# Fused attention and feed-forward block: a slot's projection in two halves instead of four quarters

## The reference

```python
# x: [8, 512, 512]; 16 heads of 32
qkv = einsum('bsh,oh->bso', x, w_qkv)          # q, k, v
scores = einsum('bhqd,bhkd->bhqk', q, k) / sqrt(32)
probs = softmax(where(causal, scores, min))
attn = einsum('bhqk,bhkd->bhqd', probs, v)
x = layernorm(x + attn @ w_o.T)
# feed-forward: 512 -> 4096 -> 512, weights unpacked from 4-bit codes and scales
x = layernorm(x + (gelu(x @ Wg.T) * (x @ Wu.T)) @ Wd.T)
```

## Time and profile before

| | before |
|---|---|
| median of 3 runs | 2690.54 us (2690.24 to 2692.3) |
| the profiled execution | 2689.03 us |
| its span in the profile | 2687.2 us |
| PE busy | 2629.9 us, 98% |
| DVE busy | 1555.0 us, 58% |
| ACT busy | 1103.5 us, 41% |
| POOL busy | 825.7 us, 31% |
| PE busy at scores (L430), 512 matmuls | 209.8 us |
| PE busy at transposes of probabilities (L438), 1280 matmuls | 228.3 us |

### The profile page before, as it was taken

The page is one execution under the profiler, slowest core; times in us unless marked ns, Lnnn a source line. Parts: engine busy times, 40 slices in busy tenths (PEclk is TensorE's granted clock), DMA queues, the critical chain, the costliest instruction groups (busy, mean ns, idle before and its releaser), DMA issues.

```text
span 2687.2 us, 37714 instructions
## 1 busy us (share of the span) xinstructions
PE 2629.9 (98%) x13314; PEld 2148.2 (80%) x13314; DVE 1555.0 (58%) x3224; ACT 1103.5 (41%) x2518; POOL 825.7 (31%) x992
## 2 busy tenths in 40 slices
PE   7999999999789999999999999999999999999998
PEld 6777887778468888888888888888888888888886
DVE  5777777777789888876333333633333363333334
ACT  4666666666644444443222222322222232222221
POOL 2444444443634443434111111321111132111112
PEclk9999999999899999999999999999999999999999
DMA  9666876768365655565444333554344345433441
GB/s 251 188 178 178 215 212 174 190 187 233 105 250 216 225 208 204 205 262 232 163 180 189 156 141 145 210 201 172 143 182 169 141 160 229 167 141 141 182 171 48
DMA packets 143085, 493.52 MB, mean 184 GB/s; under 512 B 11568, under 2 KB 48560, under 8 KB 118320
## 3 DMA queue, kind: packets, MB, share of 16 engines
q1 hardware_dynamic: 142896, 491.11, 53.2%
HBM read 356.84 MB, written 134.22 MB: 183 GB/s over the span
## 4 chain that ended last, share of the span: by engine, by line
PE 71%; DVE 1%; DMA 1%; issue 1%; ACT 0%; POOL 0%; SPq 0%; POOLq 0%; DVEq 0%; ACTq 0%
PE bank L1038 23%; PE bank L1039 23%; PE bank L1040 23%; PE bank L452 0%; DMA scale<-down_scales 0%; DMA x1T_scratch<-x_late 0%; DVE bstats L1486 0%; PE bank L438 0%; DVE acc L1429 0%; ACT probs L562 0%; PE bank L462 0%; PE bank L419 0%; ACT bx_h L1169 0%; DVE bits L1389 0%; DVE y L708 0%
## 5 line engine op out<-in xcount | busy, mean ns | idle before, releaser
L1648 POOL TENSOR_TENSOR inter_l<-hid,inter_h 128x512 fp32r<-128x512 f32 x256 | 338.0, 1321 | 1361.5 <-ACT inter_h L1169 1361.5
L1429 DVE TENSOR_TENSOR acc<-acc,bank 128x512 f32<-128x512 f32 x512 | 350.0, 685 | 331.8 <-PE bank L1040 322.8
L1038 PE MATMUL bank<-wd,inter_h 128*128 128x512 f32 x1024 | 399.7, 390 | 6.2 <-DVE acc L1429 5.2
L1039 PE MATMUL bank<-wd,inter_h 128*128 128x512 f32 x1024 | 398.9, 390 | 0.0
L1040 PE MATMUL bank<-wd,inter_l 128*128 128x512 f32 x1024 | 398.9, 390 | 0.0
L743 POOL TENSOR_SCALAR probs<-probs,row_inv 128x128 f32<-128x128 f32 (+3 forms) x512 | 264.4, 538 | 363.1 <-DVE row_inv L664 363.1
L1448 DVE TENSOR_TENSOR hid<-hid,bank 128x512 f32<-128x512 f32 x192 | 131.8, 687 | 397.1 <-PE bank L1040 395.4
L1038 PE MATMUL bank<-bx_h,wg 128*128 128x512 f32 x896 | 349.4, 390 | 0.9 <-ACT u_g L1169 0.9
L1039 PE MATMUL bank<-bx_l,wg 128*128 128x512 f32 x896 | 349.1, 390 | 0.0
L1040 PE MATMUL bank<-bx_h,wg 128*128 128x512 f32 x896 | 349.1, 390 | 0.0
L1038 PE MATMUL bank<-bx_h,wu 128*128 128x512 f32 x896 | 348.7, 389 | 0.0
(11 more groups left out here) (139 smaller groups left out, 4357.9 us busy)
## 6 DMA issues: line engine op xcount, KB each, us to landing
wg<-w_scratch SPq DMA_DIRECT2D x48, 1792.0 KB, 9.0
wu<-w_scratch SPq DMA_DIRECT2D x48, 1792.0 KB, 12.9
wd<-w_scratch SPq DMA_DIRECT2D x48, 1024.0 KB, 4.9
q_st<-qk_scratch SPq DMA_DIRECT2D x128, 256.0 KB, 5.0
k_st<-qk_scratch SPq DMA_DIRECT2D x128, 256.0 KB, 6.9
w_scratch<-wg SPq DMA_DIRECT2D x16, 1792.0 KB, 8.2
w_scratch<-wu SPq DMA_DIRECT2D x16, 1792.0 KB, 10.0
qk_scratch<-q_stage SPq DMA_DIRECT2D x32, 512.0 KB, 3.6
```

Source lines behind the costliest of these rows:

```text
L1038: pe.matmul(out, a(0), b(0), start=start, stop=False, skip_group_check=True)
L1039: pe.matmul(out, a(0), b(1), start=False, stop=False, skip_group_check=True)
L1429: dve.tensor_tensor(a, a, d_bank[n % 2][:, :], ALU.add).then_inc(d_added, 1)
L1648: pool.tensor_tensor(inter[1][:, m, t, :], hid[:, 2 * m + t, :], f32(inter[0][:, m, t, :]), ALU.subtract).then_inc(inter_split, 1)
```

## The change

In TensorE's loop over `k`, the four quarters of a slot's projection are placed behind S1 (the first two) and S3 (the last two), where one stood behind each of S0, S1, S2 and S3. The order in a slot becomes S0 T0, S1 P P T1, S2 T2, S3 P P T3, with V directly behind S0 where a slot has one. The waits that stood ahead of each entry move with it. No instruction is added or removed, and nothing changes on the other engines.

```diff
                     for k in range(TT):
                         if cur:
                             scores(b, s, k)
-                        for kind, n, use, c in pieces[k * len(pieces) // TT:(k + 1) * len(pieces) // TT]:
+
+                        half = len(pieces) // 2
+                        for kind, n, use, c in {1: pieces[:half], 3: pieces[half:]}.get(k, ()):
                             if b == 0 and c == 0 and s < OUT_SLOT:
```

## The result

The kernel with halves takes 2727.97 us in the median (2727.51 to 2728.72, 4 runs) against 2690.39 us (4 runs) of the kernel before: a ratio of 1.0140, with a 95% interval of 1.0123 to 1.0158. It is slower by 37.6 us, where 39.5 were forecast (2730 against 2690.5). Its profiled execution took 2727.51 us, with a span of 2725.7 us.

What follows compares the result with a forecast made beforehand. PE, busy 98% of the span, was taken as the bound. Six regular batches at 5.58 us (33.5) plus 3.16 each for batches 0 and 7 made 39.8; on 2689.03 that gives 2728.8, predicted 2730; 8-in-10 range 2712 to 2738.

Steps and rivals of the forecast that it cites:

- the nine slots named: Attention slots 1, 2, 4, 6, 8, 9, 10, 13 and 14, where PE should wait at T2 or S3.
- added wait = 0.70 + 0.06 - slack: S3's wait for the mask of S1: 0.53 us in slots 2, 8, 9, 10, 14; 0.25 in 1, 4, 6, 13.
- The term that was a little off: Where DVE's last mask held back the residual sum, under 0.1 us per slot could be regained; waits were counted in full.
- 3.16: Added us in each of batches 0 and 7, from fewer or different waiting slots than a regular batch.
- the sum: Six regular batches at 5.58 us (33.5) and batches 0 and 7 at 3.16 each: together 39.8 us.
- V and slot 12: V waits 0.41 us for ACT's copy in slots 3, 7, 11; T0 of slot 12 adds 0.70: 1.23 and 0.70 a batch.
- That the delay is swallowed at S2 of the next slot: Rival: S3's delay partly comes back at the next slot's S2; 24 us in all, 2714 us; chance 0.13.
- That nothing or a gain comes: Two rivals: DVE's copy and mask start earlier too, 2695 or 2690 (chance 0.05); old waits go, 2680 (chance 0.03).
- That the clock falls: Rival: granted clock falls to 0.83 over the six regular batches, time about 2835 us; chance 0.02.
- the busy time would stay: Sign for the profile after: engines' busy time unchanged, with PE idle ahead of T2 or S3 in nine slots.

Runs made afterwards that it cites:

- second_pair: Against the kernel before, only the second pair of quarters joined (behind S0, S1, S3 and S3): 2716.02 us, ratio 1.0094.
- short statistics: Residual-row statistics read 128 of 512 features: 2719.75 us on the kernel with halves (2727.97 with full statistics), 2688.01 us on the kernel with quarters.
- first_pair: Against the kernel before, only the first pair of quarters joined (behind S1, S1, S2 and S3): 2703.89 us, ratio 1.0049.
- four_slots: Kernel before with quarters behind S0, S1, S1, S3 in slots 2, 10, 14 and S0, S0, S1, S3 in slot 12: 2686.04 us, ratio 0.9985.

## Why the prediction was right

**The mechanism.** The chain from the end of the last quarter over DVE's projection work, the mask of S0 and the copy of T0 to the mask of S1 does not start sooner, and S3 does. The slot-by-slot table shows it in the nine slots named, and in no other; second_pair holds all of it and short statistics take away just what they shorten. The rule "added wait = 0.70 + 0.06 - slack" gave 0.53 and 0.25. Measured were 0.54, 0.48, 0.49, 0.45 and 0.56 in slots 2, 8, 9, 10 and 14, and 0.24 to 0.26 in 1, 4, 6 and 13.

**The term that was a little off.** Slots 8 to 10 give 1.42 together instead of 1.59. This is what the prediction had bounded by under 0.1 a slot and then left out: the residual sum now starts 0.20 behind T3 (344.25 against 344.05) where it was 0.27 (327.70 against 327.43), since it had been held by the mask of S3 and no longer is. V waits 0.41 by its distance from S0, but its slots are only 0.36 to 0.37 longer. With this the six regular batches grew by 32.3 us instead of 33.5. Up to S0 of batch 1 the kernel after is 3.2 us later (111.33 against 108.15) and behind batch 6 it takes 3.0 us more, where 3.16 were forecast for each of batches 0 and 7. That the first of these fits so well is in part luck: in the kernels with unmoved quarters batch 1 starts anywhere between 108.15 and 108.80. Together the profiled executions are 38.5 us apart (2725.7 against 2687.2) where the sum said 39.8. The other 0.9 us between this and the medians' 37.6 lies in which executions were profiled: the one before was 1.4 us below its median, and the prediction carried this over, and the one after only 0.5.

**V and slot 12** came as worked out, and by first_pair from the quarter that had stood ahead of them.

**A wait that the description of DVE's order left out.** DVE's mask of S0 also waits for T3 of the slot before. T3 stands behind the last quarter, which did not move, so this wait starts from the same point as the chain and leaves the account as it is.

**The rivals.** That the delay is swallowed at S2 of the next slot: slot 10 kept its wait at S2 (S1 to S2 was 1.71 and is 2.32 with one quarter of 0.70 more between, so 0.1 less), and slots 2 and 14 kept theirs (1.44 and 1.42, now 2.13 in both). That nothing or a gain comes: the copy of T0 started at its old time. That the clock falls: it stayed at 1.00 in each window above, with longer waits in thirteen slots of a batch. The Trainium skill ("TensorE: Matmul & The Clock Gate", A second HAM failure mode) describes, for a bf16 kernel, a clock that swings when TensorE idles shortly and often between groups of matmuls that cycle through PSUM banks. The windows of this kernel do not show it.

**What was read wrongly ahead of time.** I said that the busy time would stay and that the waits would show as idle ahead of S3. Of the 5.4 us by which a regular batch grew, PE's busy time holds 3.0 (88.92 against 85.92) and only 2.4 is idle. T2 and S3 in slot 8 have no idle beside them in the rows above, though S3 comes 0.49 late.

## What to carry to other kernels

When work is moved on an engine that never idles, list for each instruction that comes sooner what it waits for, and read from the timeline how early that result is; counting how much work lies between a buffer's two uses is not enough, because a chain on another engine can start from the end of something that did not move. In this nearly full engine each new wait cost nearly its full length in every batch. Before a quarter of work is moved into a gap, look also at what stands behind each consumer on the other engines. Two quarters behind S1 in every slot cost 9.6 us; in slots 2, 10 and 14 alone, where the gap was, they gained about 0.2 us a batch, and most of the 4.5 us of four_slots came from slot 12, where T0 had waited.

## What the runs showed of the hardware

A short wait of TensorE need not appear as idle time in this profile. The ends of matmuls are modelled past the next start: one of 256 to 512 columns is drawn 0.36 to 0.48 us long, and where nothing is waited for the next instruction starts 0.20 to 0.32 behind it. So a wait of up to about 0.16 us hides behind the modelled end of the matmul ahead, and where two such waits follow each other, as at T2 and S3, 0.49 us show as 0.13 (from the end of S2 at 341.86 to T2 at 341.99). In the two profiled executions a span longer by 38.5 us came with 23.8 us more of PE busy time for the same 13314 matmuls. The Trainium skill says in "Perfetto Trace Analysis", Identifying the Most-Contended Engine, that the busy share of matmuls is not a good measure of how close a kernel is to the roofline. This trace agrees in that the busy time grew by 23.8 us with no work added. Here the distance between starts gave a slot's length to within some 0.04 us from batch to batch, with single exceptions of up to 0.4.
